# Attention stage of a two-layer kernel: residual add ahead of the next tile's statistics, one-time work placed anew

## What is computed

```python
x = x + _L0_xattn_ref(_layernorm(x), ctx, ctx, Wq, bq, Wo, bo)     # 16 heads, causal softmax attention
x = x + _L0_ffn_ref(_layernorm(x), centroids, expert_biases, Ws_up, Ws_down, W_up, W_down)  # 64 experts, top 8, sigmoid gates
x = x + _L1_xattn_ref(_layernorm(x), ctx, ctx, Wq, bq, Wk, bk, Wv, bv, Wo, bo)  # autocorrelation by FFT
x = x + _L1_ffn_ref(_layernorm(x), weight, ln_gamma, ln_beta)      # ternary weights, quantised input

def _L0_xattn_ref(q, k, v, Wq, bq, Wo, bo):
    qh, kh, vh = (proj_split(q), proj_split(k), proj_split(v))      # one Wq, bq for all three
    scores = jnp.einsum('bhqd,bhkd->bhqk', qh, kh) / scale          # then the causal mask
    weights = jax.nn.softmax(scores, axis=-1)
    attn = jnp.einsum('bhqk,bhkd->bhqd', weights, vh)
    return concat @ Wo + bo
```

## Time and profile before

| what | value |
|---|---|
| median of 3 runs (lowest to highest) | 1265.1 us (1264.62 to 1271.6) |
| the profiled execution, own time | 1266.42 us |
| its span, first to last instruction | 1264.6 us |
| PE / DVE / ACT / POOL busy, share of the span | 96 / 84 / 73 / 61 % |
| mean granted TensorE clock | 0.992 |
| first row maximum (tile 0) / last (tile 63) | 13.80 / 293.75 us |
| first matmul of the experts | 304.91 us |

### The profile page before, as it was taken

One profiled execution on the slowest core, in us unless ns is written; L12 is line 12 of the kernel. 1 busy time (PEld: TensorE's weight loads), 2 busy tenths in 40 slices (PEclk: granted clock), 3 DMA queues, 4 the chain that ended last, 5 costly groups with the idle time before them and its releaser, 6 DMA issues. The chain is left out here.

```text
span 1264.6 us, 28435 instructions
## 1 busy us (share of the span) xinstructions
PE 1214.1 (96%) x9881; PEld 997.0 (79%) x9881; DVE 1061.9 (84%) x2053; ACT 920.0 (73%) x1600; POOL 766.2 (61%) x829
## 2 busy tenths in 40 slices
PE   7899999998999999999999999999999999899976
PEld 5677777776888888888888888888888888799965
DVE  5989999895887978978978979879879887689986
ACT  4689898886777776777777777777777776777761
POOL 4766766662755755665656656656656633577773
PEclk9999999998999999999999999999999999999998
DMA  5511111104787677777677776776776786111004
GB/s 127 112 32 29 33 29 34 32 24 101 175 186 181 170 186 173 181 174 177 177 170 178 184 177 169 180 177 169 185 178 166 183 189 164 38 31 34 18 2 133
DMA packets 126174, 159.99 MB, mean 127 GB/s; under 512 B 20840, under 2 KB 59504, under 8 KB 126064
## 3 DMA queue, kind: packets, MB, share of 16 engines
q1 hardware_dynamic: 120750, 156.06, 51.2%
q10 hardware_dynamic: 5314, 2.53, 0.7%
HBM read 152.25 MB, written 6.29 MB: 125 GB/s over the span
## 5 line engine op out<-in xcount | busy, mean ns | idle before, releaser
L1147 ACT ACTIVATE e_pu<-e_pu 128x1024 f32<-128x1024 f32 x256 | 258.7, 1010 | 203.3 <-PE e_pu L1183 203.1
L1084 DVE TENSOR_TENSOR e_m<-e_pu,raw 128x1024 f32<-128x1024 f32 x256 | 310.0, 1211 | 94.0 <-ACT e_pu L1147 93.9
L1004 POOL TENSOR_TENSOR e_ml<-e_m,e_mh 128x1024 fp32r<-128x1024 f32 x80 | 192.5, 2407 | 145.9 <-ACT e_mh L1157 144.4
L1157 ACT CAST e_mh<-e_m 128x1024 fp32r<-128x1024 f32 x256 | 267.3, 1044 | 4.9 <-DVE e_m L1084 4.9
L1089 DVE TENSOR_TENSOR e_ml<-e_m,e_mh 128x1024 fp32r<-128x1024 f32 x176 | 241.0, 1369 | 25.7 <-ACT e_mh L1157 25.7
L1181 PE MATMUL e_pu<-r_xh,wuh 128*128 128x512 f32 x528 | 214.7, 407 | 0.7 <-PEq L211 0.7
L1183 PE MATMUL e_pu<-r_xl,wuh 128*128 128x512 f32 x528 | 209.3, 396 | 0.0
L1193 PE MATMUL e_py<-e_mh,wdl 128*128 128x512 f32 x528 | 209.2, 396 | 0.0
L1182 PE MATMUL e_pu<-r_xh,wul 128*128 128x512 f32 x528 | 209.2, 396 | 0.0
L1192 PE MATMUL e_py<-e_mh,wdh 128*128 128x512 f32 x528 | 208.1, 394 | 0.0
L1196 PE MATMUL e_py<-e_ml,wdh 128*128 128x512 f32 x528 | 167.3, 395 | 0.1
(11 more groups left out here) (225 smaller groups left out, 2351.1 us busy)
## 6 DMA issues: line engine op xcount, KB each, us to landing
raw<-gates_scratch SPq DMA_DIRECT2D x512, 256.0 KB, 4.3
x_res<-in_x_dram SPq DMA_DIRECT2D x64, 64.0 KB, 1.9
xcT<-in_ctxT_dram SPq DMA_DIRECT2D x64, 64.0 KB, 2.0
held<-in_ctx_dram SPq DMA_DIRECT2D x32, 128.0 KB, 2.1
raw<-in_L_ffn_W_up_dram SPq DMA_DIRECT2D x4, 512.0 KB, 4.7
raw<-in_L_ffn_W_down_dram SPq DMA_DIRECT2D x4, 512.0 KB, 5.6
gates_scratch<-raw SPq DMA_DIRECT2D x16, 128.0 KB, 2.3
out_dram<-t_res SPq DMA_DIRECT2D x8, 256.0 KB, 3.0
```

The lines of the kernel that those rows point to most:

```text
L1004: nc.gpsimd.tensor_tensor(flat(ml[k][:]), flat(m[k][:]), flat(mh[k][:]).bitcast(F32), ALU.subtract).then_inc(m_low[1], 1)
L1084: nc.vector.tensor_tensor(flat(m[r % 3][:]), flat(pu[r % 3][:]), flat(gt[i % SPREAD]), ALU.mult).then_inc(gated, 1)
L1147: nc.scalar.activation(flat(pu[k][:]), flat(pu[k][:]), ACT.Silu).then_inc(silued, 1)
L1157: nc.scalar.copy(flat(mh[k][:]), flat(m[k][:])).then_inc(m_high, 1)
```

## The change

1. DVE list: `add_out` moves ahead of `stats_of` and `aggregate`.
2. PE: `turn_probs` does two transposes instead of four, `turn_probs_on` six instead of four; `turn_in` between them therefore comes two blocks earlier. The first half is still signalled after four.
3. POOL: a `low_part` of 264 columns in every loop step instead of 528 in every second one.
4. POOL: the ten bias operations leave steps 8 to 13 for steps 48 to 51 and 57 to 60; `norms.norm` of the first chunk is cut into `roots` (step 12), `centre` (13) and `scale` (14).
5. DVE: the one-time work moves to places behind `aggregate` and ahead of `row_max` (steps 4 to 11), or behind the step; `boe` and `centT` come in step 3. PE's one-time work moves a step earlier and behind the stages of its step. SP issues `Wo`, `bo` and the centroids (`third`) in step 1, ahead of x of tile 2; they leave ACT's queue.
6. Start: `ones` and `mhalf` are set first; ACT runs one Exp ahead of its second group of loads; PE runs nine fp32 128x128 matmuls of ones (`WARMING`) before it waits for its first inputs.
7. End: the gates are turned and copied in step 66 instead of 65, behind the last `scores`.

```diff
+WARMING = 9
-        second = [hmask, maskk, maskq, Wo, bo, centroids]
+        second = [hmask, maskk, maskq]
+        third = [Wo, bo, centroids]
...
                     sp.dma_start(xcT[:, r, 1, :], ctxT[:, bass.ds(t * P, P)]).then_inc(loaded[r], 16)
+                    if isinstance(t, int) and t == 1:
+                        for dst, src in third:
+                            sp.dma_start(dst, src).then_inc(third_landed, 16)
...
-                order = ((invert_sum, 6), (scale_out, 6), (shift, 4), (norm, 1), (stats_of, 0), (aggregate, 0),
-                         (add_out, 6), (route, 0), (row_max, 3))
+                order = ((invert_sum, 6), (scale_out, 6), (shift, 4), (norm, 1), (add_out, 6), (stats_of, 0),
+                         (aggregate, 0), (route, 0), (row_max, 3))
...
+                late = {4: weight_sums, 5: weight_mean, 6: weight_inverse, 7: weight_round, 8: weight_upper, 9: weight_lower}
...
+                    if isinstance(t, int) and t == 5:      # behind turn(t, r)
                         dve.wait_ge(o_bias_made, 1)
                         nc.vector.tensor_copy(braw[:, 2:4, :], p_bias...).then_inc(o_bias_out, 1)
...
                 def low_part(t, k):
-                    cols = bass.ds((t // 4 - peeled // 4) * piece, piece)
-                    wait_apart(pool, high, t + 2 * k + 2, idle["pool"])
+                    cols = bass.ds((t // 4 - peeled // 4) * piece + (k % 2) * (piece // 2), piece // 2)
+                    wait_apart(pool, high, t + k + 1, idle["pool"])
...
-                        norms.norm(pool, x_res, cst["mhalf"], 0, idle["pool"])
-                    if not isinstance(t, int) and r % 2 == 1:
-                        low_part(t - r, r // 2)
+                        norms.roots(pool, cst["mhalf"], 0, idle["pool"])
+                    if isinstance(t, int) and t == 13:
+                        norms.centre(x_res, 0)
+                    if isinstance(t, int) and t == 14:
+                        norms.scale(pool, 0, idle["pool"])
+                    if not isinstance(t, int):
+                        low_part(t - r, r)
...
-                bias_parts = {8: bias_high, 9: bias_rest, 10: bias_middle, 11: bias_add, 13: bias_low}
+                bias_parts = {looped: bias_high, looped + 1: bias_rest, looped + 2: bias_first, looped + 3: bias_middle,
+                              looped + 9: bias_add, looped + 10: bias_add_on, looped + 11: bias_low, looped + 12: bias_low_on}
...
+                    act.wait_ge(preset_dve, 1)
+                    nc.scalar.activation(warm[:], cst["mhalf"][:], ACT.Exp)
...
                 def turn_probs(t, r):
-                    for j in range(4):
+                    for j in range(2):
...
                 def turn_probs_on(t, r):
+                    for j in range(2, 4):
+                        ins = nc.tensor.transpose(ppT[:, j, :], prob[...], cst["ident"][:])
+                    ins.then_inc(p_turned, 1)
...
                     if isinstance(t, int) and t == 0:
+                        pe.wait_ge(preset_dve, 1)
+                        for k in range(WARMING):
+                            nc.tensor.matmul(ps[:, k % 4, 0:2]..., cst["ones"][:], cst["ones"][:], start=True, stop=True)
...
-                    if isinstance(t, int) and t == n_tiles + 1:
+                    if isinstance(t, int) and t == n_tiles + 2:
                         pe.wait_ge(v_out, n_tiles)
                         routing.turn_gates(pe, pj, 0)
```

More of the change, by code:

```diff
@@ L300, in route @@
                         return
+                    if t in late:
+                        late[t]()
+                    if t == 10:
+                        at_least(dve, added, 4)
+                        norms.take_stats(x_res, 0)
+                    if t == 11:
+                        norms.aggregate(dve, 0, idle["dve"])
                     if t == looped + 5:
@@ new lines, in weight_mean, with weight_inverse @@
+                def weight_mean():
+                    dve.wait_ge(w_summed, 1)
+                    nc.vector.tensor_scalar(cst["beta"][:], p_beta, 1.0 / (D * D), None, ALU.mult).then_inc(w_chain, 1)
+                    dve.wait_ge(w_chain, 2)
+                    nc.vector.tensor_scalar(wrec[:], cst["beta"][:], 1e-5, None, ALU.add).then_inc(w_chain, 1)
+                def weight_inverse():
+                    dve.wait_ge(w_chain, 3)
+                    nc.vector.reciprocal(wabs[:], wrec[:]).then_inc(w_chain, 1)
@@ new lines, in weight_round, with weight_upper, weight_lower @@
+                def weight_round():
+                    dve.wait_ge(w_chain, 4)
+                    nc.vector.tensor_scalar(cst["wt"][:], wt_raw, wabs[:], 1.5 * 2 ** 23, ALU.mult, ALU.add).then_inc(w_chain, 1)
+                def weight_upper():
+                    dve.wait_ge(w_chain, 5)
+                    nc.vector.tensor_scalar(cst["wt"][:], cst["wt"][:], 1.5 * 2 ** 23, 1.0, ALU.subtract, ALU.min).then_inc(w_chain, 1)
+                def weight_lower():
+                    dve.wait_ge(w_chain, 6)
+                    nc.vector.tensor_scalar(cst["wt"][:], cst["wt"][:], -1.0, None, ALU.max)
@@ new lines, in _ @@
+                late = {4: weight_sums, 5: weight_mean, 6: weight_inverse, 7: weight_round, 8: weight_upper, 9: weight_lower}
+                def step(t, r):
+                    if isinstance(t, int) and t == 3:
+                        dve.wait_ge(bias_made, 1)
+                        nc.vector.tensor_copy(cst["boe"][:], ppT[:, 0, :])
+                        nc.vector.tensor_copy(cst["centT"][:], ppT[:, 1, 0:E]).then_inc(bias_out, 1)
+                    turn(t, r)
+                    if isinstance(t, int) and t == 0:
+                        dve.wait_ge(first_landed, 16 * len(first))
+                        nc.vector.tensor_copy(bqB[:], cst["bqc"][:].to_broadcast([P, P])).then_inc(broadcast, 1)
+                    if isinstance(t, int) and t == 1:
@@ L332, in step @@
-                    if isinstance(t, int) and t == 5:
[L333 to L338, removed]
+                    if isinstance(t, int) and t == 5:
@@ L348, in step @@
[L348 to L356, removed]
@@ L555, in scores @@
                     at_least(pe, keys, t + 1)
+                    if isinstance(t, int) and t == 0:
+                        pe.wait_ge(masked, 1)
                     for half in range(2):
@@ L625, in step @@
                     if isinstance(t, int) and t == 0:
+                        pe.wait_ge(preset_dve, 1)
+                        for k in range(WARMING):
+                            nc.tensor.matmul(ps[:, k % 4, 0:2].rearrange("p h k -> p (h k)"), cst["ones"][:], cst["ones"][:],
+                                             start=True, stop=True)
                         pe.wait_ge(first_landed, 16 * len(first))
-                    if isinstance(t, int) and t == 3:
-                        pe.wait_ge(second_landed, 16 * len(second))
+                    if isinstance(t, int) and t == 5:
+                        pe.wait_ge(bias_out, 1)
+                        pe.wait_ge(w_out, 1)
+                    if isinstance(t, int) and t == 6:
+                        pe.wait_ge(o_bias_out, 1)
+                    turn(t, r)
+                    if isinstance(t, int) and t == 2:
+                        pe.wait_ge(third_landed, 16 * len(third))
                         pe.wait_ge(broadcast, 1)
-                        pe.wait_ge(preset_dve, 1)
                         nc.tensor.matmul(ppT[:, 0, :], bqB[:], cst["Wo"][:], start=True, stop=False)
@@ L686, in norm, with roots @@
     def norm(self, pool, x_res, half, c, idle):
+        self.roots(pool, half, c, idle)
+        self.centre(x_res, c)
+        self.scale(pool, c, idle)
+    def roots(self, pool, half, c, idle):
         ops = self.nc.gpsimd
```

61 lines of the change are left out of this document (27 added, 34 removed).

## The result

The changed kernel takes 1259.96 us (median of six runs, 1257.56 to 1260.44), the kernel before 1267.45 in the same set. The ratio is 0.9927 with a 95% interval of 0.9909 to 0.9944: faster by 0.6 to 0.9%, under the 1% that the prediction called a change. The median of 1259.96 is 0.5 above the predicted range, but the kernel before took 2.3 more in this set than the 1265.1 us that the prediction started from; on those the ratio gives 1255.9 us, inside the range and 3.7 above the 1252.2. So the measured gain is about half of the 12.9 us that the prediction summed up. The profiled execution has 1260.20 us and a span of 1258.4, 6.2 less than the span before.

What follows compares the result with a forecast made beforehand. Bounds: in the loop a two-tile ring through `weigh`, `row_max` and `add_out`; ahead of it POOL's one-time operations. Gains 2.5 + 7.4 + 4.2 - 1.2 = 12.9 us, against 1265.1 giving 1252.2 us; range 1244 to 1259.5.

Steps and rivals of the forecast that it cites:

- rival 2: Loop: the halves give back what the earlier `add_out` wins, 4.27 a tile as before, 1256.4 us; chance 0.25.
- its own signs: Loop: `norm` 0.4 to 0.7 every step; wrong if `norm` stays at 0.34 or PE waits for `kx`.
- The sign for the steps ahead of the loop: Ahead of the loop: no stretch of granted clock 0.5 between 56 and 66 us.
- so DVE goes on when `kx` ends ... The two alternate: 8.28 for two, 4.14 a tile: Loop: `kx` holds `norm`; steps of 4.09 and 4.19 alternate, 4.14 a tile instead of 4.27, gaining 4.2 us.
- the 4.09: Loop, held step: `add_out` 3.40 behind `aggregate`, then 0.69 over the statistics to the next `aggregate`.
- Rival 3's condition: Loop: if `norm` issues first, `kx` and the scores wait; 4.68 a tile at full waits, 1269.5 us; chance 0.04.
- 0.6, counted at the end: Steps 50 to 52, where routing shares the ACT copy: the earlier input copy gives 0.2 each.
- `project` hardly waits: Loop: `project` hardly waits for the input copy, so bringing it 0.22 forward was priced only in steps 50 to 52.
- the 1.4 to 1.6 plus 2: First steps: 1.4 to 1.6 by tile 3 from moving the chain, another 2 from warm matmuls; 2.5 taken.
- the chain: First steps: step 5's chain moves behind the scores, `weigh` waits for its end (L340) at 24.5.
- another 2: First steps: gain if the nine warm matmuls bring PE to full pace before its first inputs.
- the other routing steps, `aggregate` 0.1 nearer to `row_max`: +0.4: Behind the loop: a cost of 0.4 in the remaining routing steps, within the stretch's net +1.2.

Runs made afterwards that it cites:

- e3: Changed kernel with POOL's half low part moved behind the keys and waiting for the end of `norm`: ratio 0.9887, loop 131.90 us.
- e4: Changed kernel with POOL's half low part moved right behind the keys, without waiting for `norm`: ratio 0.9881, loop 131.64 us.
- e1: Changed kernel with whole low parts of 528 columns in every second loop step again, `add_out` still first: ratio 0.9972, loop 142.99 us.
- e2: Changed kernel with the old DVE order (`stats_of`, `aggregate`, then `add_out`) in every step, halves kept: ratio 0.9882, loop 134.98 us.
- e12: Changed kernel with `turn_in` behind four transposes of the probabilities again, not two: ratio 0.996, loop 140.32 us.
- e9: Changed kernel with the old DVE order everywhere, the loop's half low part behind `norm`, and the bias product earlier in step 5: ratio 0.9875.
- e10: Changed kernel with new DVE order only in the loop, old outside, half low part behind `norm`, bias product earlier in step 5: ratio 0.9842.
- e8: Changed kernel with the bias operations back in steps 8 to 13 and the first chunk's norm whole in step 12: ratio 1.0025.
- e7: Changed kernel without the nine warm matmuls of ones: ratio 0.9932.
- e5: Changed kernel without POOL's ten bias operations (`bias_parts` not called): ratio 0.9926, tiles 45 to 63 in 80.31 us.
- e11: e10 with POOL's bias pieces and those of the chunk's norm also behind `expand`, waiting for `norm`: 1246.84 us, ratio 0.9828.
- e6: Changed kernel with the bias product ahead of `scores` in step 5 and its copy ahead of `row_max`: ratio 0.9901.

## Why the prediction was right, and where not

**The total: right by the width of its range.** 12.9 us of gain were summed up and 6.2 came. The time agrees with rival 2's 1256.4 (1255.9 on the prediction's own starting time), and the range took that rival in, but the cause is not the one that the rival named. By its own signs the prediction failed in the loop: PE waits there for `kx`, and `norm` stays at 0.34 in every second step. The distance from tile 63 to the experts moved too. The sign for the steps ahead of the loop came true: the granted clock was 1.00 from 56 to 66.

**The loop: wrong, 4.2 us of gain against none.** The step that failed is the sum "so DVE goes on when `kx` ends ... The two alternate: 8.28 for two, 4.14 a tile". Its POOL terms are right to 0.05, and the step with the hold took the 4.09 that it gave (155.65 to 159.74). But `norm` was held (0.61 to 0.72) in two of four steps, not in every one. The sum had the keys act through the hold on `norm` and through one late `weigh`, and read the time at which `norm` is ready against a `row_max` that doesn't move. The late keys themselves push `row_max` (0.88 behind the masks), and with it the next `norm`, `aggregate` and keys: the ring of 8.40 and 8.67, where 8.28 was summed up. e3 and e4 settle it: with the keys earlier the loop gains 4.7 and 5.0 us, and no less where `norm` is held in every step. Here the prediction leaned on the Trainium skill, page SBUF — State Buffer, section Who interferes with whom: the exclusion of the two operations is seen in every step of e4 (0.45 to 0.72 against 0.34), but that it costs anything doesn't follow from it. Rival 2, "the halves give back what the earlier `add_out` wins", came true in its size; in its cause it was the other way round, for e1 shows the halves winning 6.4 and e2 the earlier `add_out` losing 1.6. Rival 3's condition never arose: `kx` issued first.

**Edit 2: wrong in the loop.** It was priced at "0.6, counted at the end", and with "`project` hardly waits" in the loop. The row was right for the kernel before; edit 1 took the slack that it showed. e12 measures 3.7 in the loop and 0.6 behind it. An edit priced alone against the rows of before misses what another edit of the same change does to it.

**Ahead of the loop: right, 6.6 of 7.4.** The 0.8 missing is there in e2, e9 and e10 (41.3 to 41.5): it is edit 1 again, 0.9 to 1.1. The prediction named POOL's place ahead of the keys as the bound, and e8 confirms it with 13.0 us. That is more than the 11.4 of the ten operations: the granted clock fell as well. DVE's moved pieces (edit 5) were priced at 0.04 to 0.64 each; no run undid that edit.

**First steps: right in size, by two errors.** 2.6 against 2.5. Tile 2 came 5.65 earlier, far more than the 1.4 to 1.6 plus 2 that the parts gave; then L377 behind the row maximum was late. The prediction had seen that the chain moves behind the scores and that `weigh` waits for it, put its end at 24.5 (it was 22.06), and did not see the clock fall behind the wait. The warm matmuls brought 0.7 at tile 2 in the changed kernel (20.52 against 21.20 in e7) and nothing at tile 3. The "another 2" for a full pace before the first inputs is about the 2.3 by which tile 0 came earlier in e3, but that was one execution of twelve, and the whole isn't slower without them (e7).

**Behind the loop: right in sign, -2.9 against -1.2.** The bias operations were priced at 2.3 and cost about 2 (e5). The term that was mis-sized is "the other routing steps, `aggregate` 0.1 nearer to `row_max`: +0.4": edit 1 costs 2.8 in this stretch (e2; 2.6 in e10). `add_out` in front puts the variance 0.3 later, and here POOL has long pieces ahead of the keys. One step has 1.25 of it: in step 53 PE waits 1.31 for the keys, which stand on POOL behind three routing pieces of 0.4 to 0.9; in e2, e9, e10 and e11, with the old order there, and before the change this wait is absent. In steps 57 to 60 of the changed kernel `norm` is held on top:

```profile
258.09 1.57 POOL L492 TENSOR_SCALAR s_bpart<-held,ident 3x512 bf16<-3x512 f32 x1
259.64 1.03 POOL L405 TENSOR_TENSOR kx<-qkT,hmask 128x512 f32<-128x512 f32 x1
```

```profile
259.81 0.95 DVE L273 TENSOR_SCALAR a_xn<-x_res,a_mv,a_rstd 128x128 f32<-128x128 f32 x1
```

Edit 7 gave 1.15 (from tile 62 to 63 it took 4.55 instead of 5.70) where 0.9 was predicted; no run undid it.

Tile 63 to the experts was predicted unchanged and took 0.4 more in the changed kernel. The runs fall in two groups, whatever was edited: 11.4 to 11.55 in the changed kernel, e5, e6, e7 and e10, and 11.09 to 11.10 in all others. In the first the granted clock was down to 0.50 before the first matmul of the experts, and the last `out_project` took 0.79 instead of 0.49. Why the clock falls earlier in that group stays open. The stretch from 2.9 to 0.9 us ahead of that matmul, in the changed kernel and in e2:

```profile
296.00:298.00 2.00, 0.97 (x4) 0.67 (x3) 0.55 (x2) 0.27 (x1) 0.00 (x0) 0.68 1.06 229
```

```profile
290.00:292.00 2.00, 0.97 (x17) 0.68 (x14) 0.55 (x2) 0.53 (x3) 0.00 (x0) 1.00 1.02 224
```

**What stays open.** With the keys out of the way the loop stops at 4.11. Between 100 and 190 us of e3 PE was busy 88.56 of 90 us and ACT 86.50, with hardly a gap from one input copy of ACT to the next. One of the two is the likely next bound, but no run tested which.

## What to carry to other kernels

When an operation that others wait for (here the masked keys) shares an engine's queue with work that nobody waits for, put that work behind it, even where this makes another engine's instruction slower; then ask of every wait, not how long it is, but whether the ring that sets the pace runs through it. Price the edits of one change together: a reorder that shortens one ring takes the slack that two others were measured against. And an order that is right in a loop need not be right in the steps around it, where the same stages stand beside other work.

## What the runs showed of the hardware

- The wait for L377 (1.10 us, 0.95 in e3) was followed by a fall of the granted clock (0.62 at 24 to 28 us in the changed kernel, which mixes the levels of 1.2 and 2.4 GHz) only where PE had come up to its pace by 14.0 us: five executions of five, none of the four others. Nine fp32 matmuls of ones, about 4 us long and ending at 5.0 to 5.3, brought that pace up before 5.6 us in one execution and after 18.7 in three.
- In e7 the granted clock reads 1.00 from 12 to 20 us, while `project` took 1.22 (14.78) against 0.60 in the loop: PE's slow pace at the start isn't in that column of the profile, and only the durations show it.

```profile
12.00:16.00 4.00, 3.65 (x40) 2.30 (x38) 2.67 (x4) 1.63 (x7) 1.04 (x1) 1.00 0.50 128
```

```profile
14.78 1.22 PE L640 MATMUL pj<-xcT,Wq 128*128 128x256 f32 x2 [0.35 <-ACT xcT L527]
```

- POOL takes as long for few partitions as for many: of the same kind of operation (`TENSOR_TENSOR`) on 512 columns, those of the bias on 3 partitions take 1.15 us, `kx` on 128 partitions 1.03 to 1.05.
